# Graph-attention layer on one core: the node pass looks three pairs ahead, stores one result, and the feed-forward pass rebuilds normalised rows

## The reference, cut to what matters

```
x = x + gnn(layernorm(x)) + mix(layernorm(x))
z = layernorm(x)                       # z = (x - m) / sqrt(v + eps)
weight = z @ wr + br                   # one number a node
chosen = the 6249 nodes of largest weight
y = gelu(z[chosen] @ w1 + b1) @ w2 + b2
x = x + z;  x[chosen] += y * weight[chosen]
```

## Time and profile before

| | us |
|---|---|
| median of 3 runs | 3194.72 (3194.56 to 3195.56) |
| the profiled execution, its own time | 3195.1 |
| its span in the profile | 3193.3 |
| PE busy | 2129.0 (67%) |
| DVE busy | 1907.1 (60%) |
| POOL busy | 2109.1 (66%) |
| ACT busy | 731.0 (23%) |

### The profile page before, as it was taken

One profiled execution on the slowest core, in us unless ns is written; L12 is line 12 of the kernel. 1 busy time (PEld: TensorE's weight loads), 2 busy tenths in 40 slices (PEclk: granted clock), 3 DMA queues, 4 the chain that ended last, 5 costly groups with the idle time before them and its releaser, 6 DMA issues.

```text
span 3193.3 us, 38619 instructions
## 1 busy us (share of the span) xinstructions
PE 2129.0 (67%) x8271; PEld 1513.0 (47%) x8271; DVE 1907.1 (60%) x4819; ACT 731.0 (23%) x2199; POOL 2109.1 (66%) x2189
## 2 busy tenths in 40 slices
PE   4547458866667676566767767676762455269998
PEld 3335235544444444444544545444541111158887
DVE  7995458877777777655555555555553677742222
ACT  2224231211111111022222222222210455222221
POOL 4727667777777777777777777777772777144443
PEclk9679678988888888788888888888886788579999
DMA  5537644444444444555555555555553788211111
GB/s 172 151 110 235 105 113 125 126 123 125 124 126 124 124 125 123 132 145 152 152 152 152 153 152 153 154 152 155 150 130 73 211 259 258 85 30 59 53 56 45
DMA packets 259969, 426.67 MB, mean 134 GB/s; under 512 B 73682, under 2 KB 165748, under 8 KB 259764
## 3 DMA queue, kind: packets, MB, share of 16 engines
q0 software_dynamic: 96592, 260.07, 31.5%
q1 hardware_dynamic: 163300, 165.80, 16.4%
HBM read 337.21 MB, written 88.48 MB: 133 GB/s over the span
## 4 chain that ended last, share of the span: by engine, by line
POOL 37%; PE 22%; issue 18%; DVE 15%; DMA 4%; ACT 2%; DVEq 1%; ACTq 1%; POOLq 1%; SPq 0%
POOL G L1234 30%; PE bank L2033 7%; PE bank L916 5%; PE bank L925 5%; DMA G<-tab_d,sidx 3%; POOL G L1211 2%; DVE G L1645 2%; PE bank L1984 2%; POOL rows_d L1218 1%; PE bank L2014 1%; POOL acc L581 1%; POOL G L591 1%; DVE shared L1563 1%; PE bank L611 1%; DVE acc L1661 1%
## 5 line engine op out<-in xcount | busy, mean ns | idle before, releaser
L1234 POOL DMA_INDIRECT G<-tab_d,sidx x1632 | 1549.9, 950 | 517.9 <-issue 481.7
L2033 PE MATMUL bank<-G,ident 128*128 128x264 f32 x3264 | 919.0, 435 | 606.2 <-DVE G L1645 524.0
L2033 PEld LDWEIGHTS bank<-G,ident 128*128 128x128 f32 x3264 | 655.0, 212 | 867.4 <-issue 520.0
L1645 DVE TENSOR_TENSOR G<-G,bank 128x1024 f32<-128x1024 f32 x408 | 491.5, 1215 | 1.8
L1661 DVE TENSOR_TENSOR acc<-acc,bank 128x264 f32 x816 | 348.2, 427 | 192.6 <-PE bank L2033 158.4
L1900 ACT ACTIVATE bank<-work 128x196 f32<-128x196 f32 x51 | 17.2, 338 | 1210.9 <-DVE work L1632 1210.9
L2014 PE MATMUL bank<-kvw,shared 128*128 128x512 f32 x392 | 190.1, 631 | 42.2 <-DVE shared L1563 31.1
L1616 DVE CAST work<-penI 128x64 f32 (+1 forms) x51 | 11.2, 220 | 323.4 <-DMA G<-tab_d,sidx 320.3
L1984 PE MATMUL bank<-G,acc 128*128 128x264 f32 x392 | 133.5, 498 | 97.3 <-DVE acc L1374 75.8
L611 PE MATMUL bank<-G,ident 128*128 128x512 f32 x98 | 78.1, 890 | 157.1 <-POOL G L593 157.1
L889 POOL DMA_INDIRECT out<-G,acc x49 | 48.9, 999 | 193.0 <-DVEq L1004 183.4
(11 more groups left out here) (398 smaller groups left out, 3111.9 us busy)
## 6 DMA issues: line engine op xcount, KB each, us to landing
G<-tab_d,sidx POOLq DMA_INDIRECT x1632
acc<-x_in SPq DMA_DIRECT2D x98, 256.0 KB, 4.1
shared<-xnT_d SPq DMA_DIRECT2D x98, 256.0 KB, 4.0
accP_d<-acc SPq DMA_DIRECT2D x100, 132.0 KB
tab_d<-acc SPq DMA_DIRECT2D x49, 260.0 KB, 3.4
xnT_d<-acc SPq DMA_DIRECT2D x49, 256.0 KB, 2.2
mix_d<-acc SPq DMA_DIRECT2D x49, 256.0 KB, 3.0
G<-mix_d SPq DMA_DIRECT2D x49, 256.0 KB, 4.3
```

What stands on the lines that cost most here:

```text
L1234: g.indirect_dma_start(out=G[:, s, t, 0:TR], out_offset=None, in_=tab_d, in_offset=bass.IndirectOffsetOnAxis(ap=sidx[:, s, t:t + 1], axis= ...
L1645: v.tensor_tensor(gm[:, q4], gm[:, q4], W1[:, q4][:, :, :, None].to_broadcast([P, 4, HG, CG]), ALU.mult).then_inc(g_ready, 1)
L2033: last = te.matmul(bank[1 + i % NSB][:, 0:ROW], ident[:, :], G[:, s, i * IT + k, :], start=(k == 0), stop=(k == IT - 1))
```

## The change

Three things are done at once.

1. `weights_of` runs three pairs ahead rather than two, with four buffers for the factors rather than two. ACT's `exponent(q + 1)` is issued ahead of the logarithm of pair q rather than behind it.
2. z is no longer made or stored in the node pass. DVE takes the dot product from x2 of the same pair, and corrects it in the choice with 1/sqrt and shift of each node. The pass keeps 1/sqrt (`inv`) and shift (`shift_n`) of all nodes in SBUF. In the choice, DVE turns them into two numbers a node, which SP stores to a small table `norm_d` (8 bytes a node).
3. In the feed-forward pass, POOL gathers the rows of `out` in place of z, and two more indirect DMAs a tile gather the two numbers a node. ACT then makes z from both in place (`make_z`), ahead of gelu in its queue. PE's transposes wait for ACT.

```diff
             def node_weight(q):
                 wk = Chain(dve, vnw, 2 * q)
-                dve.wait_ge(z_ready, q + 1)
                 for t in (0, 1):
-                    wk(v.scalar_tensor_tensor(junk, zz[:, q % 2, t, :], 1.0, wr_ps, ...
+                    wk(v.scalar_tensor_tensor(junk, x2[:, q % 2, t, :], 1.0, wr_ps, ...
...
-                if q + 2 < NP:
-                    weights_of(q + 2)
-                if q:
-                    node_weight(q - 1)
+                if q + 3 < NP:
+                    weights_of(q + 3)
+                node_weight(q)
                 dve.wait_ge(v_std, q + 1)
-                v.tensor_reduce(mv2[:, s, :, 3], mv2[:, s, :, 1:3], AX, ALU.add)
-                ck(v.scalar_tensor_tensor(mv2[:, s, :, 0], mvp[:, s, :, 0], -1.0, mv2[:, s, :, 1], ALU.mult, ALU.mult))
+                c = slice(2 * q, 2 * q + 2)
+                v.tensor_scalar(inv1[:, c], inv[:, c], 1.0, None, ALU.add)
+                ck(v.scalar_tensor_tensor(shift_n[:, c], mvp[:, s, :, 0], -1.0, inv[:, c], ALU.mult, ALU.mult))
...
# node_act
+                if q + 1 < NP:
+                    exponent(q + 1)
                 act.wait_ge(v_var, q + 1)
                 a.activation(var2[:, s, 0:2], mvp[:, s, :, 1], ACT.Ln, bias=epsn).then_inc(v_log, 1)
-                if q + 1 < NP:
-                    exponent(q + 1)
...
-                for t in (0, 1):
-                    a.activation(zz[:, s, t, :], x2[:, s, t, :], ACT.Identity, ...
...
# node_loads (SP)
-                sp.dma_start(z_v[q], zz[:, q % 2, :, :]).then_inc(b_out[q % 2], 16)
                 sp.dma_start(out_v[q], bb[:, q % 2, :, :]).then_inc(b_out[q % 2], 16)
...
# threshold_dve, start; and ahead of its wait for cnt_sum
+            lk(v.tensor_tensor(wnode[:, :], wnode[:, :], inv, ALU.mult))
+            lk(v.scalar_tensor_tensor(wnode[:, :], shift_n, wr_sum, wnode[:, :], ALU.mult, ALU.add))
...
+            dve.wait_ge(z_ready, NP)
+            lk(v.reciprocal(inv1, inv1))
+            lk(v.tensor_tensor(stat[:, :, 1], shift_n, inv1, ALU.mult))
+            lk(v.tensor_tensor(stat[:, :, 0], inv, inv1, ALU.mult))
+            v.sem_inc(norm_ready, 1)
             dve.wait_ge(cnt_sum, 1)
...
+            lk(v.scalar_tensor_tensor(norm_i[:, 0:NT2], perm_l, float(NB), bank[6][:, 0:NT2], ALU.mult, ALU.add))
             v.sem_inc(perm_ready, 1)
...
# ffn_pool
+            def gather_z(q):
+                gather(zl, out, q, z_in)
+                for t in tiles(q):
+                    g.indirect_dma_start(out=nl[:, q % 2, t, :], out_offset=None, in_=norm_d,
+                                         in_offset=rows_at(q, t, norm_i)).then_inc(z_in[q % 2], 16)
...
# ffn_pe, turn
-                pe.wait_ge(z_in[s], 32 * u + 16 * len(tiles(q)))
+                pe.wait_ge(z_made, q + 1)
...
# ffn_act
+            def make_z(q, s, u):
+                act.wait_ge(z_in[s], 64 * u + 32 * len(tiles(q)))
+                for t in tiles(q):
+                    last = a.activation(zl[:, s, t, :], zl[:, s, t, :], ACT.Identity, bias=nl[:, s, t, 1:2], scale=nl[:, s, t, 0:1])
+                last.then_inc(z_made, 1)
...
+            def body(q, s, first, u):
+                if u is not None:
+                    make_z(q + 2, s, u)
                 for j in range(FC // 2):
                     act.wait_ge(f_up, 4 * q + j + 1)
```

More of the change, by code:

```diff
@@ L99, in gps_kernel @@
         mix_d = nc.dram_tensor("mix_d", [NP, P, 2 * D], FP32).ap()
-        z_d = nc.dram_tensor("z_d", [NPAD, D], FP32).ap()
+        norm_d = nc.dram_tensor("norm_d", [P * NB, 2], FP32).ap()
         bank = [ctx.enter_context(nc.psum_tensor(f"bank{i}", [P, 512], FP32)) for i in range(8)]
@@ L378, in gps_kernel @@
         xpl, xm_in = slots(4), slots(4)
-        t1, uu, x2, zz, bb = (slots(2) for _ in range(5))
+        t1, uu, x2, bb = (slots(2) for _ in range(4))
         junk = gpiece(D)
@@ L382, in gps_kernel @@
         bst2 = gpiece(12)
-        mv2 = gpiece(16).rearrange("p (s t k) -> p s t k", s=2, t=2)
-        epsn = gpiece(1)
+        epsn, wr_sum = gpiece(1), gpiece(1)
         dsum = gpiece(2 * HG).rearrange("p (t h) -> p t h", t=2)
-        rec, wrc = (gpiece(4 * HG).rearrange("p (s t h) -> p s t h", s=2, t=2) for _ in range(2))
+        inv, inv1, shift_n = (Gf[:, k * NB:k * NB + NB] for k in range(2 * CT * ROW // NB - 3, 2 * CT * ROW // NB))
+        rec, wrc = (gpiece(8 * HG).rearrange("p (s t h) -> p s t h", s=4, t=2) for _ in range(2))
         assert go[0] <= 2 * CT * ROW
@@ L527, in weights_of @@
                 aq = acc[:, 2 * q:2 * q + 2, D:ROW]
-                if q >= 2:
-                    dve.wait_ge(u_scaled, q - 1)
+                if q >= 4:
+                    dve.wait_ge(u_scaled, q - 3)
                 ck(v.tensor_tensor(dsum, aq[:, :, 0:HG], aq[:, :, HG:2 * HG], ALU.add))
-                ck(v.reciprocal(rec[:, q % 2], dsum))
-                v.tensor_tensor(wrc[:, q % 2], aq[:, :, HG:2 * HG], rec[:, q % 2], ALU.mult).then_inc(rec_ready, 1)
+                ck(v.reciprocal(rec[:, q % 4], dsum))
+                v.tensor_tensor(wrc[:, q % 4], aq[:, :, HG:2 * HG], rec[:, q % 4], ALU.mult).then_inc(rec_ready, 1)
             def node_weight(q):
                 wk = Chain(dve, vnw, 2 * q)
-                dve.wait_ge(z_ready, q + 1)
                 for t in (0, 1):
-                    wk(v.scalar_tensor_tensor(junk, zz[:, q % 2, t, :], 1.0, wr_ps, ALU.mult, ALU.mult, accum_out=wnode[:, 2 * q + t:2 * q + t + 1]))
-            v.memset(mv2[:, :, :, 2], 1.0)
+                    wk(v.scalar_tensor_tensor(junk, x2[:, q % 2, t, :], 1.0, wr_ps, ALU.mult, ALU.mult, accum_out=wnode[:, 2 * q + t:2 * q + t + 1]))
             v.memset(epsn, EPS)
@@ L543, in node_dve @@
             dve.wait_ge(wr_placed, 1)
-            weights_of(0)
-            weights_of(1)
+            v.tensor_reduce(wr_sum, wr_ps, AX, ALU.add)
+            for q in range(3):
+                weights_of(q)
             for q in range(NP):
@@ L627, in node_act @@
                 s = q % 2
+                if q + 1 < NP:
+                    exponent(q + 1)
                 act.wait_ge(v_var, q + 1)
                 a.activation(var2[:, s, 0:2], mvp[:, s, :, 1], ACT.Ln, bias=epsn).then_inc(v_log, 1)
-                if q + 1 < NP:
-                    exponent(q + 1)
                 act.wait_ge(v_log, q + 1)
-                a.activation(mv2[:, s, :, 1], var2[:, s, 0:2], ACT.Exp, scale=-0.5).then_inc(v_std, 1)
+                a.activation(inv[:, 2 * q:2 * q + 2], var2[:, s, 0:2], ACT.Exp, scale=-0.5).then_inc(v_std, 1)
                 act.wait_ge(zs_ready, q + 1)
                 if q >= 2:
-                    act.wait_ge(b_out[s], 32 * (q // 2))
-                    act.wait_ge(vnw, 2 * q - 2)
+                    act.wait_ge(b_out[s], 16 * (q // 2))
                 for t in (0, 1):
-                    a.activation(zz[:, s, t, :], x2[:, s, t, :], ACT.Identity, bias=mv2[:, s, t, 0:1], scale=mv2[:, s, t, 1:2])
-                for t in (0, 1):
-                    last = a.activation(bb[:, s, t, :], x2[:, s, t, :], ACT.Identity, bias=mv2[:, s, t, 0:1], scale=mv2[:, s, t, 3:4])
+                    b = 2 * q + t
+                    last = a.activation(bb[:, s, t, :], x2[:, s, t, :], ACT.Identity, bias=shift_n[:, b:b + 1], scale=inv1[:, b:b + 1])
                 last.then_inc(z_ready, 1)
@@ L678, in gps_kernel @@
         place_i, part_i = ppiece(NB).bitcast(I32), ppiece(NB).bitcast(I32)
-        perm_i = ppiece(2 * NQ).bitcast(I32)
+        perm_i, norm_i = (ppiece(2 * NQ).bitcast(I32) for _ in range(2))
         perm_l, keep_w = ppiece(NT2), ppiece(2 * NQ)
@@ L867, in gather @@
                                          in_offset=rows_at(q, t)).then_inc(signal[q % 2], 16)
+            def gather_z(q):
[3 more added lines that the diff above has]
+                                         in_offset=rows_at(q, t, norm_i)).then_inc(z_in[q % 2], 16)
             pool.sem_inc(y_stored, 2)
             pool.wait_ge(perm_ready, 1)
+            pool.wait_ge(norm_out, 16)
             for s in (0, 1):
-                pool.wait_ge(b_out[s], 32 * ((NP - s + 1) // 2))
+                pool.wait_ge(b_out[s], 16 * ((NP - s + 1) // 2))
             for q in (0, 1):
-                gather(zl, z_d, q, z_in)
+                gather_z(q)
                 gather(bl, out, q, b_in)
@@ L877, in ffn_pool @@
             pool.wait_ge(w_made, 1)
-            gather(zl, z_d, 2, z_in)
+            gather_z(2)
             for q in range(NQ):
@@ L882, in ffn_pool @@
                     pool.wait_ge(w_made, q + 2)
-                    gather(zl, z_d, q + 3, z_in)
+                    gather_z(q + 3)
                 pool.wait_ge(f_y, q + 1)
@@ L954, in ffn_act @@
             a = nc.scalar
+            def make_z(q, s, u):
[3 more added lines that the diff above has]
+                last.then_inc(z_made, 1)
+            make_z(0, 0, 0)
+            make_z(1, 1, 0)
             act.wait_ge(f_in, 64)
-            def body(q, s, first):
```

(14 more changed lines are left out.)

23 lines of the change are left out of this document (11 added, 12 removed).

## The result

| | before | after |
|---|---|---|
| median, 7 runs each | 3195.15 us (3194.56 to 3197.18) | 3205.23 us (3200.54 to 3206.81) |
| ratio to before, 95% interval | | 1.003, 1.0018 to 1.0041 |
| profiled execution, its span | 3195.1, 3193.3 us | 3200.54, 3198.7 us |

A forecast was written before the change was run, and what follows sets the result against it. The node pass was taken as bound by a loop between engines, the feed-forward pass by PE. Against the profiled 3195.1 us, -28.2 - 2.5 + 1.4 + 24.8 + 6.1 = +1.6; forecast 3196.3, range 3170 to 3223.

The forecast's parts named there:

- the likeliest case: The whole change: 3196.3 us, two large effects that cancel, with its own range 3189 to 3204; chance 0.59.
- Loop of the node pass: Node pass: a POOL-ACT-DVE loop sets 5.1 us a pair; factors three pairs ahead give 4.53, gain 28.2 us.
- a reduction of two elements that becomes a scalar addition: Node pass: DVE's ten steps a pair stay the same but for this swap, which was costed at nothing.
- the prediction's own sign of being wrong: Wrong if feed-forward turns stay 14.26 us apart, or x2 starts in the node pass come 4.7 or more apart.
- End of the pass and choice: End of the node pass and the choice behind it: a gain of 2.5 us, then a loss of 1.4.
- Tiles: Feed-forward pass: z is made 1.8 us too late, two tiles take 31.0 against 28.5, loss 24.8 us.
- the landing: Feed-forward pass: a tile's last small gather lands in 2.6 us; tile loss 18.8 with 2.0, 49 with 5.0.
- Start of the pass: Feed-forward pass: PE's second turn waits for the tenth gather, not the sixth, then for ACT; loss 6.1 us.
- hidden gathers: Rival, feed-forward pass: the gathers stay hidden since POOL has room in each tile; 3171.5 us, chance 0.13.
- a landing of 5.0: Rival, feed-forward pass: a gather of 8-byte rows lands as late as one of 32 bytes; 3223 us, chance 0.08.
- a falling clock: Rival, feed-forward pass: PE's clock falls in the stalls, 2.5 us each; 3221, or 3246 with all 20; chance 0.08.
- The node pass gains only half: Rival, node pass: something else binds, likeliest the DMA engines; 4.8 us a pair, 13 short, 3209; chance 0.12.

The follow-up runs named there:

- experiment 2: Kernel before with only the factors three pairs ahead in four buffers, z still stored, on a slower chip: ratio 0.9914 to before, node pass 217.39 us.
- experiment 8: Kernel before with only the factors three pairs ahead, z still stored, on the usual chip: 3162.19 us, ratio 0.9909 to before.
- experiment 1: Changed kernel with the small addition's 1 read from PSUM in a two-operand addition: node pass 217.95 us against 226.53, ratio 1.0012 to before.
- experiment 7: Kernel before with 49 gathers of 8-byte rows, which nobody reads, added behind those of z: 3198.43 us, ratio 1.0023 to before.
- experiment 10: Changed kernel with the 1 of the two-operand addition read from PSUM, a repeat run: node pass 217.95 us, ratio 1.0019 to before.
- experiment 5: Changed kernel with the 1 read from PSUM and POOL's gathers a tile earlier: 3173.41 us, ratio 0.9944 to before.
- experiment 4: Changed kernel with `make_z` of tile q+2 moved behind gelu of tile q: turn 3 to turn 24 315.63 us, ratio 1.0016 to before.
- experiment 3: Changed kernel with POOL's gathers a tile earlier: turn 3 to turn 24 300.31 us against 318.65, ratio 0.9989 to before.
- experiment 9: Changed kernel with the addition of 1 written with two operands, the 1 in SBUF: node pass 226.57 us, ratio 1.0026 to before.
- experiment 11: Changed kernel with POOL's gathers a tile earlier, run again for its total: turn 3 to turn 24 299.42 us, ratio 0.9971 to before.

## Why the prediction was nearly right, step by step

The forecast was 3196.3; measured were 3205.23. That is inside the range (3170 to 3223), but 1.2 us above the likeliest case's own (3189 to 3204), and "slower by over 0.2%" had a chance of 0.32 against 0.50 for "same". By stages the forecast was +1.6 us and the table gave +9.4. That it came this near is partly luck: the node pass and the drain were 9.7 and 4.2 us worse than forecast, the tiles and the start of the pass 5.5 and 1.1 better.

- **Loop of the node pass: right in mechanism.** Factors three ahead end it (experiments 2 and 8). The free interval of 4.53 read from the earlier trace rows is what experiments 2 and 8 measured, 4.53 and 4.52 on average.
- **The step that failed**: "a reduction of two elements that becomes a scalar addition; I cost that at nothing". It costs 0.16 us itself (315 less 159 ns), and DVE now sets the pace: 226.53 - 217.95 = 8.6 us in all (experiment 1). Most pairs come 4.67 apart rather than 4.53; the first interval, with the addition of 2346 ns, takes 6.70 rather than 4.51 and is 2.2 of the 8.6. By the prediction's own sign of being wrong (4.7 or more apart) this part failed: the mean is 4.72. The product that it waits for stands in the earlier trace rows for one pair, but the rows of before alone didn't show the danger: 30 of the 49 reductions there start while a product runs, and none took over 160 ns. The 1.1 us left are about what four intervals of 4.87 to 4.89 in experiment 1 add.
- **End of the pass and choice**: -2.3 and +1.7, for -2.5 and +1.4. The reciprocal of 98 columns takes 0.77, not 0.5.
- **Tiles: right in mechanism, too large in size.** With time 0 again 3.37 ahead of the scatter, so at 2928.04, z is made at 15.6 (forecast 16.0), and `up` starts 0.77 later (1.15). Two tiles take 2 x 15.17 = 30.3, not 31.0, which leaves 14.0 for the rest (13.8). The mis-sized terms are the landing and `up`'s start; against them, the loss runs over 21 intervals, not 20. For the landing, the trace has a median of 2.4. The 2.4 that was worked out with the Trainium skill, "DMA: Bandwidth & Descriptors", section "Anatomy of one DMA" (2.7 less 0.3), was nearer to it than my 2.6.
- **Start of the pass**: +5.0 for +6.1. The second turn came 14.93 us after the first gather rather than 9.04, so +5.9, near the forecast. From there to turn 3 it took 0.9 less than before, mostly in the first `up` (8.28 rather than 9.55): the granted clock rose from 0.50 to 1.00 at 2.4 us after that `up` began, and before at 5.0. That wasn't in the sum.
- **Not in the sum**: the drain, 4.2 (experiment 7).

Of the rivals, hidden gathers and a landing of 5.0 are out. So is a falling clock, for the changed kernel as it was: it stayed 1.00 from 2817.4 to 3189.4, through stalls of under 1 us. In four of its variants it did fall once, as told next. "The node pass gains only half" came out in size, 4.7 apart, though not by the DMA engines: their share was 0.81, and at 0.97 in experiment 8 they didn't bind.

Explained only in part: from turn 2 to turn 3 the changed kernel and its variants took between 14.3 and 18.7 us, and one and the same kernel 17.38 and 15.76 (experiments 1 and 10). In all six variants on the two other chips ACT stood 3.13 to 4.39 us ahead of its third gelu activation; on the usual chip (the changed kernel and experiment 5) it didn't. What held it stays open: the profile names no engine of this core, or a matmul. PE, which waits for that gelu, then stood too: for 4.85 us ahead of turn 2 in experiment 4, and inside `up` of tile 1 in the others, for up to 1.25 us at a time. In experiments 3, 9 and 11 the granted clock fell to 0.50 just behind this, for 3.4 us, and PE was busy for 16.8 us from turn 2 to turn 3, where it was 14.7 in the changed kernel. In experiments 1 and 10 it stayed at 1.00 through stalls of 0.84 and 1.25 us.

## What to carry to other kernels

When an edit swaps one tiny instruction for another of the same size, look at what GpSimd does at that moment, and keep one operand of it in PSUM if it can be. The DMAs added at the end of each tile's row cost the tiles nothing while nobody waited for them, and once somebody did, their whole lateness counted; ask for such a DMA a tile sooner before judging its price. When three edits go in together, time each alone: here one of them was worth 0.9% alone, and all three together were 0.3% slower.

## What the runs showed of the hardware

- A DVE addition of 128x2 waits for GpSimd's running product when its operands are all in SBUF (315 ns as a scalar addition, 302 with two operands; 168 and 160 at least), and doesn't with one in PSUM (159 in all 49). The reduction of before, all in SBUF but with one input, didn't wait either (158 to 160). At the start of the pass a multiplication with two operands in SBUF took 4.30 us, which can be the same wait, over four products that POOL ran from 2478.62 to 2482.66:

```profile
2478.40 4.30 DVE L530 TENSOR_TENSOR G<-acc,G 128x8 f32<-128x8 f32 x1
2478.62 1.06 POOL L587 TENSOR_TENSOR G<-acc,G 128x512 f32<-128x512 f32 x1
...
2481.62 1.04 POOL L589 TENSOR_TENSOR G<-G 128x512 f32<-128x512 f32 x1
```

  The Trainium skill, "SBUF — State Buffer", section "SBUF: two separate sides", says that VectorE and GpSimd share a pair of ports that one instruction holds to its end, and that a VectorE instruction with two SBUF inputs or in a two-port mode needs it. Experiments 1, 9 and 10 agree for the two-operand form. That the scalar addition ran in such a mode no run here shows; its wait of 315 ns would follow from it.
- An indirect DMA takes POOL 0.94 us and 0.30 to the next, for rows of 8 bytes as of 1 KB, and lands 2.4 us after its issue, against 2.7 for 1 KB.
- POOL's drain at the end of the program grew from 3.57 to 7.73 us with 49 small gathers more, in the changed kernel and in experiment 7.
- In the six variants of the changed kernel that ran on the two other chips, ACT stood 3.13 to 4.39 us ahead of its third gelu activation, for a reason that stays open, and in experiments 3, 9 and 11 the granted clock fell to 0.50 for 3.4 us, 0.6 to 0.8 us after that stall ended.
